# Layer norm statistics over two interleaved row tiles, with the engines' orders laid out anew

## What is computed

```python
# layer 0..3
x = _layernorm(x + _L0_gnn_ref(x, L0_gnn_a, adj, adj), axis=-1)   # pair attention, normalised over all pairs
x = _layernorm(x + _L1_gnn_ref(x, adj, ...), axis=-1)             # GAT, then GIN with a two layer MLP
x = _layernorm(x + _L2_gnn_ref(x, adj, W, e, bias), axis=-1)      # graph convolution, fixed attention
x = _layernorm(x + _L3_gnn_ref(x, adj, W, a_src, a_dst), axis=-1) # GAT with elu
# with
m = jnp.mean(x, axis=axis, keepdims=True)
v = jnp.var(x, axis=axis, keepdims=True)
return (x - m) / jnp.sqrt(v + eps)
```

## Time and profile before

| | us |
|---|---|
| runs: median (lowest to highest of 3) | 1191.42 (1190.25 to 1193.15) |
| profiled execution: span from first to last instruction | 1188.6 |
| PE busy (matmul) | 1103.5, 93% |
| DVE busy | 1055.8, 89% |
| ACT busy | 964.7, 81% |
| POOL busy | 594.6, 50% |
| six norms on DVE: bn_stats, 768 instructions | 166.8 |
| six norms on DVE: bn_aggr, 768 instructions | 71.7 |

### The profile page before, as it was taken

The page is one execution under the profiler, slowest core; times in us unless marked ns, Lnnn a source line. Parts: engine busy times, 40 slices in busy tenths (PEclk is TensorE's granted clock), DMA queues, the critical chain, the costliest instruction groups (busy, mean ns, idle before and its releaser), DMA issues.

```text
span 1188.6 us, 28920 instructions
## 1 busy us (share of the span) xinstructions
PE 1103.5 (93%) x7752; PEld 907.9 (76%) x7752; DVE 1055.8 (89%) x3894; ACT 964.7 (81%) x2453; POOL 594.6 (50%) x1250
## 2 busy tenths in 40 slices
PE   4779999999999999999999999999999999999964
PEld 3457777888777888887778888877778888788743
DVE  6887999999999999999999999999999899997642
ACT  3566888888888888888888889888888898888753
POOL 4243435555564555556555555555545554553422
PEclk7799999999999999999999999999999999999976
DMA  3010001110011111000111110101111010010000
GB/s 76 19 36 19 27 28 46 31 31 22 22 35 35 35 35 35 26 28 17 35 35 35 35 35 26 35 9 35 35 35 35 29 37 30 17 46 10 28 9 19
DMA packets 59478, 36.17 MB, mean 30 GB/s; under 512 B 3872, under 2 KB 54816, under 8 KB 59424
## 3 DMA queue, kind: packets, MB, share of 16 engines
q1 hardware_dynamic: 59424, 35.54, 10.0%
HBM read 18.75 MB, written 8.39 MB: 23 GB/s over the span
## 4 chain that ended last, share of the span: by engine, by line
PE 58%; POOL 10%; issue 9%; DVE 5%; ACT 2%; DMA 1%; POOLq 0%; SPq 0%; ACTq 0%; DVEq 0%
PE ps L965 14%; PE ps L893 7%; PE ps L949 6%; PE ps L982 4%; PE ps L1025 4%; PE ps L934 4%; PE ps L744 4%; PE ps L737 3%; POOL rirA L559 2%; PE ps L1014 2%; PE ps L880 2%; PE ps L1043 2%; PE ps L1042 2%; PE ps L919 1%; DMA xA<-in_x_dram 1%
## 5 line engine op out<-in xcount | busy, mean ns | idle before, releaser
L965 PE MATMUL ps<-hE,pTE 128*128 128x128 f32 x1024 | 131.0, 277 | 0.2
L982 PE MATMUL ps<-gin_j,hgat 128*128 128x512 f32 x256 | 124.4, 610 | 3.0 <-DVE gin_j L1495 1.8
L965 PE MATMUL ps<-hB,pTB 128*128 128x128 f32 x1024 | 125.3, 275 | 0.7 <-DVE pTB L1626 0.6
L893 PE MATMUL ps<-xsA,pA 128*128 128x128 f32 x1024 | 124.4, 275 | 0.0
L965 PEld LDWEIGHTS ps<-hE,pTE 128*128 128x128 f32 x1024 | 122.8, 193 | 0.9 <-issue 0.6
L1025 PE MATMUL ps<-att_j,xD 128*128 128x512 f32 x256 | 122.3, 601 | 0.8 <-ACT xD L2207 0.8
L965 PEld LDWEIGHTS ps<-hB,pTB 128*128 128x128 f32 x1024 | 119.4, 192 | 1.4 <-DVE pTB L1626 1.1
L893 PEld LDWEIGHTS ps<-xsA,pA 128*128 128x128 f32 x1024 | 119.4, 192 | 0.4 <-issue 0.3
L2250 ACT ACTIVATE pA<-vA,nmA,rirA 128x512 f32<-128x512 f32 x128 | 107.0, 845 | 6.3 <-DVE vA L1683 5.3
L2312 ACT ACTIVATE pE<-wE,mnE 128x512 f32<-128x512 f32 x128 | 92.4, 723 | 20.9 <-DVE mnE L1613 20.8
L1595 DVE SCALAR_TENSOR_TENSOR wE<-ps,hE,y2E 128x512 f32<-128x512 f32 x128 | 92.1, 739 | 13.8 <-ACT y2E L2282 13.7
(11 more groups left out here) (238 smaller groups left out, 3084.6 us busy)
## 6 DMA issues: line engine op xcount, KB each, us to landing
xA<-in_x_dram SPq DMA_DIRECT2D x32, 256.0 KB, 2.9
xrA<-in_x_dram SPq DMA_DIRECT2D x32, 256.0 KB, 2.7
xrB<-xB SPq DMA_DIRECT2D x32, 256.0 KB, 2.3
out_dram<-xout SPq DMA_DIRECT2D x32, 256.0 KB, 2.3
adj_i<-in_adj_dram SPq DMA_DIRECT2D x1, 1024.0 KB, 5.5
a<-in_L_gnn_a_dram SPq DMA_DIRECT2D x2, 64.0 KB, 5.1
w_sb<-in_L_gnn_W_dram SPq DMA_DIRECT2D x2, 64.0 KB, 3.7
l2w<-in_L_gnn_W_dram SPq DMA_DIRECT2D x2, 64.0 KB, 3.2
```

What stands on the lines that cost most here:

```text
L893: last = mm(at("aggA")[:, i * P:(i + 1) * P], pA[:, j, i * P:(i + 1) * P], xsA[:, j], start=(j == 0), stop=(j == NT - 1))
L965: last = mm(at("agg" + n)[:, i * P:(i + 1) * P], att[n]["pT"][:, i, j], att[n]["h"][:, j, 0:P], start=(j == 0), stop=(j == NT - 1))
L982: last = mm(at("gin"), hgat[:, j], gin_j[:, j], start=(j == 0), stop=(j == NT - 1))
```

## The change

The statistics of two row tiles are read by one bn_stats: its source is a view that steps element by element between two tiles (`p (u d) -> p d u`), so the elements at even places are those of one tile and the elements at odd places those of the other. The six results are then count, mean and count x variance of either tile, and nothing has to be joined. `join_k` and its tiles `mv` are gone. `rstd_k` waits for bn directly, reads the mean and count x variance from `st` (with 1/128 folded into ve), and computes nm ahead of ve. For B, ve is computed on DVE in a new step `ve_B`.

The orders of all five engines, the order of setup and the banks of PSUM are laid out anew. The number of fill and drain turns and all other steps' contents are unchanged.

```diff
-        ln = {k: dict(y=sb("y_" + k, [P, NT, P]), st=sb("lnst_" + k, [P, NT, 6]), mv=sb("lnmv_" + k, [P, NT, 2]),
+        ln = {k: dict(y=sb("y_" + k, [P, NT, P]), st=sb("lnst_" + k, [P, NT // 2, 6]),
+        for k in ln:
+            moments = ln[k]["st"][:].rearrange("p h (u c) -> p (h u) c", c=3)
+            ln[k]["mean"], ln[k]["m2"] = moments[:, :, 1], moments[:, :, 2]
+
+        def two_tiles(src, half):
+
+            return src[:, half * 2 * P:(half + 1) * 2 * P].rearrange("p (u d) -> p d u", u=2)
...
         IN_BANK = [
...
+            [("pB2", 3), ("aggA", 2), ("pairA0", 1), ("z", 3)],
+            [("pB1", 3), ("xTE", 5), ("axD", 4), ("h3B", 2), ("outD", 4)],
+            [("aggB", 3), ("pE0", 5), ("tB", 2)],
+            [("sumA", 1), ("pairA1", 1), ("pairA3", 1), ("pE2", 5), ("pB0", 2)],
+            [("gin", 3), ("xTD", 4)],
+            [("pB3", 3), ("h3E", 5), ("rowsA", 1), ("pairA2", 1), ("pE3", 5)],
+            [("x2", 4), ("sqA", 1), ("pE1", 5), ("zT", 3)],
+            [("h012E", 5), ("tE", 5), ("xTB", 2), ("h012B", 2), ("aggE", 5)],
...
-            def stats_of(k, src=None):
+            def stats_of(k, src, ready):
+
                 def step(g):
-                    L = ln[k]
-                    y = src or (lambda i: L["y"][:, i])
-                    dve.wait_ge(s["y_" + k] if src is None else s["z_in_psum"], g.now)
-                    dve.wait_ge(s["nm_" + k], g.last)
-                    for i in range(NT):
-                        last = v.bn_stats(L["st"][:, i], y(i))
+                    dve.wait_ge(s[ready], g.now)
+                    dve.wait_ge(s["ve_" + k], g.last)
+                    for half in range(NT // 2):
+                        last = v.bn_stats(ln[k]["st"][:, half], two_tiles(src, half))
                     last.then_inc(s["bn_" + k], 1)
...
-                    if k == "B":
-                        pool.wait_ge(s["zzB"], g.now)
-                        pool.wait_ge(s["aggr_B"], g.now)
-                    else:
-                        pool.wait_ge(s["stats_" + k], g.now)
-                    eps = zzB[:] if k == "B" else consts[:, 2:3].to_broadcast([P, NT])
-                    pool.tensor_tensor(L["ve"][:], L["mv"][:, :, 1], eps, ALU.add).then_inc(s["ve_" + k], 1)
-                    pool.wait_ge(s["ve_" + k], g.now)
+                    pool.wait_ge(s["ve_B" if k == "B" else "bn_" + k], g.now)
                     pool.wait_ge(s["applied0_B" if k == "B" else "applied_" + k], g.last)
-                    pool.tensor_tensor(L["nm"][:], L["mv"][:, :, 0], consts[:, 3:4].to_broadcast([P, NT]),
+                    pool.tensor_tensor(L["nm"][:], L["mean"], consts[:, 3:4].to_broadcast([P, NT]),
                                        ALU.mult).then_inc(s["nm_" + k], 1)
+                    if k != "B":
+                        pool.tensor_scalar(L["ve"][:], L["m2"], 1.0 / P, LN_EPS, ALU.mult, ALU.add).then_inc(s["ve_" + k], 1)
+                        pool.wait_ge(s["ve_" + k], g.now)
...
-            def join_B(g):
+            def ve_B(g):
                 L = ln["B"]
-                dve.wait_ge(s["bn_B"], 1)
                 dve.wait_ge(s["bn_B"], g.now)
-                for i in range(NT):
-                    last = v.bn_aggr(L["mv"][:, i], L["st"][:, i])
-                last.then_inc(s["aggr_B"], 1)
+                dve.wait_ge(s["zzB"], g.now)
+                dve.wait_ge(s["rstd_B"], g.last)
+                v.scalar_tensor_tensor(L["ve"][:], L["m2"], 1.0 / P, zzB[:], ALU.mult, ALU.add).then_inc(s["ve_B"], 1)
```

1332 lines of the change are left out of this document (633 added, 699 removed), and 3 rows, old and new, of the table IN_BANK.

## The result

| | before | after |
|---|---|---|
| median of the runs (lowest to highest) | 1191.79 us (1190.25 to 1193.15, 4 runs) | 1217.49 us (1214.89 to 1219.46, 4 runs) |
| ratio, 95% interval | | 1.022 (1.0199 to 1.0241) |
| span of the profiled execution | 1188.6 us | 1214.1 us |

The account below looks back on a forecast made before the run. PE, busy 97.6% of the 26 turns, was taken to set the turn. From the 1188.6 us span, -16 (turns), -4 (start) and -4 (end) gave 1164.6, plus 2.8 to the median: 1167.4 us, range 1148 to 1192.

Parts of the forecast that it names:

- The loads' order in the turn is unchanged.: SP's loads in the pipeline turn: order taken as unchanged, with no cost in the turns' -16 us.
- rows_A and t_B, -0.56 of the -0.61 us a turn: Two PE holes in the turn: rows_A's shrinks from 0.56 to 0.3 us (-0.26), t_B's 0.31 closes (-0.30).
- (a) to (d): Four cuts before rows_A: squares_A sooner 0.5; mean_A sooner 0.2; sqA quicker 0.3; two late chain steps quicker 0.6 us.
- DVE, -2.8 us a turn: Statistics on DVE: 6.97 us a graph removed, 4.2 added; 2.8 us a turn lighter, bringing nothing by itself.
- rival 4: DVE's interleaved reads cost double, so DVE gets no lighter: 1191 us, or up to 1199; chance 0.08.
- POOL at nothing: POOL's rstd steps in the turn: costed at nothing, between -0.2 and +0.3 us a turn, with 45% idle.
- Start, -4 us: Stretch before graph 5's sum_A: 14 us less DVE work, perhaps a third on the path; -4, from -8 to +2.
- End, -4 us: Last graph's norms: 0.6 us less, five times, -3, and -1 for shorter queues; -4, from -6 to +2.
- Rival 2: Another wait on PE, for instance z_C or pT_E2, replaces the holes; turns give 0, 1183 us; chance 0.12.
- The best end of the turns, -27: Best case for the 26 turns: all 21.5 us of PE idle and the holes' hidden parts go, -27 us.

Follow-up runs that it names:

- store_before_keep: The changed kernel with one exchange in SP's turn, the store ahead of keep_xB: 1200.97 us, ratio 1.0061 to the kernel before.
- old_orders_neighbours: stats_old_orders with, in DVE's turn, mean_A ahead of bn_E, and y_A and bn_A behind offset_B: 1202.91 us, ratio 1.0065.
- start_att_and_rows: store_before_keep with the setup's head, the attention table's transposes, copies and last rows moved towards their old places, some banks changed: 1196.76 us, ratio 1.0025.
- old_start_own_banks: store_before_keep with before's start orders on all engines, two edge values in banks 4 and 6, four attention transposes in own banks: 1189.20 us, ratio 0.9954.
- stats_old_orders: The new statistics in the orders, setup and banks of the kernel before, with ve_B where join_B stood: 1194.34 us, ratio 1.000.
- before_neighbours: The kernel before, old statistics included, with mean_A ahead of bn_E and y_A, bn_A behind offset_B on DVE: 1214.52 us, ratio 1.0173.

## Why the prediction was wrong, step by step

**"The loads' order in the turn is unchanged."** This is the step that failed in the turns: forecast -16 us, measured +10.7. SP's list is unchanged in what it names and in its order, but what releases its entries moved: of a queue that issues in order, the entries ahead of the load decide too. y_C was moved past recip_A and mult_B3, keep_xB waits for y_C, and store and load stand behind it. I costed SP at nothing and named the danger only as a thing that "would make it wrong", by another path (less work on PE above the load). In its place the runs show the load leaving 0.91 us after scale_xA in place of 0.23, a hole of 1.22 us ahead of sum_A, and a turn of 34.16 us where 33.04 was forecast. Shown by two edits from two sides: 0.83 us a turn each.

**rows_A and t_B, -0.56 of the -0.61 us a turn.** The holes went as worked out, through (a) to (d): squares_A 1.22 us after sum_A, sqA 0.20, the middle step 0.23 and r2A 0.20 us, chain 5.66. By what PE streams, the two holes gave 0.35 + 0.31 = 0.66 us, a little more than forecast. Without the queue's wait the turn is 33.33, -0.32 to before, for a hole of 0.38 us still stands ahead of sum_A (in store_before_keep agg_A1 streams until 582.74, sum_A starts at 583.12): 33.65 - 0.66 + 0.38 = 33.37. So the mechanism at the two holes is right and about half of the sum came: the cycle through scale_xA, the load and the dots stood right behind the holes, which a list of PE's holes doesn't show. old_orders_neighbours shows the same danger once more: there the chain, shortened alone, brought +0.46 us a turn (34.28 against 33.82), at another wait.

**DVE, -2.8 us a turn.** The price of a bn_stats was right (0.34 against 0.345), the norms' groups fell from 7.45 to 4.70 us a graph ((166.8 + 71.7) / 32 against (145.3 + 5.2) / 32), which is -2.75; DVE's busy time fell by 2.05 only. Instructions that overlap count once in the one number and twice in the other; that this is the whole difference isn't shown. As forecast it brings nothing by itself; the run says so with 1.000.

The Trainium skill's page "SBUF — State Buffer", section "Door 1: The DMA port swizzle", has each access that crosses to a new 16-byte line pay a penalty, without a price for VectorE. The rows above show none for bn_stats on VectorE: 0.33 us from one to the next, though each element lies in another tile than the last. The double time of rival 4 was the prediction's own price, not the page's.

**POOL at nothing.** Right for the instruction count. Missed was that a lighter DVE moves large instructions beside POOL's small ones; in the old orders this lengthened the turn by 0.17 us (33.82).

**Start, -4 us; it was +13.35.** I counted DVE's work that fell away and one moved load, and took the rest of a newly laid setup at nothing ("transposes of adj some 1 us later: 0"; they came 3.3 us later, 9.79 against 6.47). This is the second step that failed. PE's idle time there rose from 33.4 to 50.2 us (a part of it may be missing records, 816 matmuls against 829). What the runs show: the head of the setup (transpose_w ahead of the counts, mask_adj beside POOL's triangles) is 4.2 us in the profiles and 0.4% in the ratios, its three moves not taken apart; the old start as a whole with matching banks is some 12 (180.68 to 168.61, and 1.0061 to 0.9954 in the ratios). The start of before itself, 165.45, is a low reading of its order: the profiles of the six other kernels with the old start and working banks have 167.2 to 169.1, so of the 13.35 us some 10 to 12 are the new order's. What stays open is where the other 7 to 8 us come from: the attention table's transposes, its rows, and the load of adj, each put back in turn, changed the start by +0.2, -0.8 and +0.5 us, none of it clear of what one profile can tell, as the wait came back a graph later. The distances say where the time lies: from graph 1 to 3 pass 69.8 us in start_att_and_rows and 63.4 in old_start_own_banks. The places of the first graphs' own steps, which differ there too, were not tried alone.

**End, -4 us; it was +1.4.** No run was made for the end. But stats_old_orders has the new statistics in before's own end orders, and it takes 141.7 us (1051.50 to 1193.2), against 140.95 in before and 142.3 in before_neighbours (1071.88 to 1214.2), which have the old statistics and the same end orders: the 4 us didn't come there either, so the new orders aren't what hid them. old_start_own_banks has 142.0 (1046.50 to 1188.5). Why nothing came stays open.

**The rivals.** Rival 2 (another wait takes the holes' place) had the right mechanism, a wrong place and no price above zero: it assumed the new wait to cost at most what the holes had. Nothing bounds it so: here 0.66 us were gained at the holes and 1.22 lost at the new wait. That is how the range ended at 1192. The best end of the turns, -27, was also summed wrongly: the 21.5 us and the hidden 0.38 us of 26 turns make 31. It doesn't touch the verdict.
